# A GRU with a mixture of experts behind it: the router's two weight parts as one 16-column product, their sums added on GpSimd

## The chip, the cores and the metric

The kernel runs on one core of a Trainium2 chip. A core has TensorE (PE: matmuls, with weight loads, PEld, beside them), VectorE (DVE), ScalarE (ACT), GpSimd (POOL) and SyncE (SP, which here only starts transfers). Each engine works through its own instructions in order; they wait for one another by semaphores. The metric is the device time of one execution in microseconds.

## The reference

```python
# x: (16, 256, 512), the hidden state h: (16, 512), 256 time steps in sequence
gi = x_t @ W_ih + b_ih ;  gh = h @ W_hh + b_hh
r = sigmoid(i_r + h_r) ;  z = sigmoid(i_z + h_z) ;  n = tanh(i_n + r * h_n)
h = (1 - z) * n + z * h
# every h is then a token of a mixture of 8 experts, 2 of them used:
logits = h / max(|h|, 1e-12) @ router_w                # router_w: (512, 8)
w, e = top_k(softmax(logits), 2) ;  w = w / sum(w)
out = x + sum over e of combine[:, e] * (h @ Wa[e] @ Wb[e])   # ranks of 128
```

## The kernel before

**Precision.** Every fp32 operand of a matmul is split in a high and a low fp16 part. A product is made of three terms, high x high, high x low, low x high (`TERMS`), added up in PSUM.

**Stages.** The 256 time steps are taken eight at a time: a block is 8 steps x 16 batch rows = 128 tokens, and there are 32 blocks (`NB`). Step n is step s = n % 8 of block i = n // 8. In each step TensorE does the recurrence first (`state_part`, L958 and L963 for the reset and candidate gates, L969 and L973 for the update gate) and then, in `beside(n)`, filler from other blocks: one expert's first product for the block before (`expert_down`, L1014), a half of an input product (`n_part`, L912), one expert's second product (`expert_up`, L1037), and input products for later steps (`pair_part`, L883). In the step s = 3 it also computes the router's sums for the block before (`route`, L988 and L994).

**The recurrence.** VectorE waits for the gates (`rh_done`), transposes them (L762), adds the halves (L765, L768, L771), and, with ScalarE's sigmoids and tanh (L616, L620, L622, L624) between, makes the new state (L774 to L789; L788 writes the fp16 high part that TensorE multiplies next, L746 the low part). TensorE's L958 of the next step waits for L788 (`hhi_ready`).

**The router.** The 16-bit high and low parts of the block's states are in `hf`, those of the router's weights in `rw`, stored as `[128, part, k, 8]`. `route(f)` makes the sum of squares of each token (L988, three matmuls of one column) and the 8 logits (L994, 4 values of k x 3 terms = 12 matmuls of 8 columns), side by side in the bank `nbank`. ScalarE copies the 9 columns to `router` (L647, `router_read`), in its own `beside` of step s = 3, ahead of `split_y` (L658, L662), which reads an expert's product out of PSUM. GpSimd then makes the inverse norm (`invert_norm`, L465, L469), and VectorE ranks the logits (`rank_experts`, L796 and L798: the largest values and their indices). GpSimd takes the gap of the two largest (`gaps`, L474, L475) and copies the indices (L477). One step later ScalarE turns the gap into the two weights (`weigh`, L653) and GpSimd places them in `comb` (`combine`, L482 to L491), by which VectorE adds each expert's product to the result (`add_expert`, L815; the first one of a block waits for `comb`).

**The order around it.** The order of each engine is written out by hand, in each engine's `beside(n)` and, for the last block, `last_experts()`. On VectorE `rank_experts` stands in step s = 3 behind `gru_step` and `add_expert` and in front of the next step's `gru_step`; up to step 17 a piece of weight splitting (L741) follows it. On GpSimd in step s = 3 the order is: `less_upper_half`, `low_y` (L458, the low part of an expert's product, which waits for both of ScalarE's `split_y` reads), `invert_norm`, `gaps`.

Of the kernel before, what the change touches and what calls it, by code (L numbers as in the profile page):

```python
# [9 lines left out]
ALU = mybir.AluOpType  # L10
ACT = mybir.ActivationFunctionType

P = 128
PART_SCALE = 128.0
PROD_SCALE = PART_SCALE * PART_SCALE


TERMS = ((0, 0), (0, 1), (1, 0))
# [5 lines left out]
def wait(eng, sem, value):  # L24
    if value > 0:
        eng.wait_ge(sem, value)


def gru_moe_kernel(nc, x, cond, W_ih, W_hh, b_ih, b_hh, router_w, Wa, Wb, out):
    B, T, D = x.shape  # L30
    NE, _, R = Wa.shape
    K = D // P
    S = P // B
    NB = T // S
# [15 lines left out]
    with ExitStack() as ctx:  # L50
        def sb(name, shape, dt=F32):
            return ctx.enter_context(nc.sbuf_tensor(name, shape, dt))

        def ps(name, shape):
            return ctx.enter_context(nc.psum_tensor(name, shape, F32))

        def sem(name):
            return ctx.enter_context(nc.semaphore(name))
# [15 lines left out]
        rw = sb("rw", [P, 2, K, NE], F16)  # L74
# [45 lines left out]
        hf = sb("hf", [P, 2, K, P], F16)  # L120
# [3 lines left out]

        sqs = sb("sqs", [P, 3, P])
        ones_bf = sb("ones_bf", [P, 1], BF16)
        router = sb("router", [P, NE + 1])
        normf = sb("normf", [P, 1])
        rnorm = sb("rnorm", [P, 1])
        top = sb("top", [P, 8])  # L130
# [17 lines left out]
        nbank = ps("nbank", [P, 4 * P])  # L148
# [69 lines left out]
        sq_step = sem("sq_step")  # L218
        logits_done = sem("logits_done")
        router_read = sem("router_read")  # L220
        top_step = sem("top_step")
        gap_ready = sem("gap_ready")
        rnorm_step = sem("rnorm_step")
# [14 lines left out]
        def upper_half(part):  # L238
            return sqs[:, part, :].bitcast(BF16).rearrange("p (c h) -> p c h", h=2)[:, :, 1]
        SQ_STEPS, TOP_STEPS, RN_STEPS, COMB_STEPS = 4, 2, 2, 4  # L240
# [52 lines left out]
        def splits_before(n):  # L293
            return sum(len(SPLITS[i][4]) for i in range(n))
# [105 lines left out]
        def _(pool):  # L400
# [27 lines left out]
            def split_x(b, half, n):  # L428
                of = slice(half * D // 2, (half + 1) * D // 2)
                pool.wait_ge(xhi_ready, b + 1)  # L430
                pool.wait_ge(x_scaled, b - 2)
                pool.wait_ge(both_parts_ready, 2 * (n + 2))
                low = nc.gpsimd.tensor_tensor(xh[:, b % 2, 1, of], x128[:, of], xh[:, b % 2, 0, of], ALU.subtract)  # L433
                low.then_inc(xlo_ready if half else xlo_begun, 1)

            def fold_squares(f, n):
                pool.wait_ge(sq_ready, f + 1)
                if n < T:
                    pool.wait_ge(both_parts_ready, 2 * (n + 2))
                nc.gpsimd.tensor_tensor(sq2[:, :], sq[:, 0:2 * P], sq[:, 2 * P:4 * P], ALU.add).then_inc(sq_step, 1)  # L440

            def add_squares(f, n):
                pool.wait_ge(sq_step, f * SQ_STEPS + 1)
                wait(pool, logits_done, f)
                if n < T:
                    pool.wait_ge(both_parts_ready, 2 * (n + 2))
                nc.gpsimd.tensor_tensor(sqs[:, 0, :], sq2[:, 0:P], sq2[:, P:2 * P], ALU.add).then_inc(sq_step, 1)

            def less_upper_half(f, part):
                pool.wait_ge(sq_step, f * SQ_STEPS + 2 + part)  # L450
                nc.gpsimd.tensor_tensor(sqs[:, part + 1, :], sqs[:, part, :], upper_half(part), ALU.subtract
                                        ).then_inc(sq_step, 1)

            def low_y(m):
                pool.wait_ge(yhi_ready, m + 1)
                pool.wait_ge(y32_ready, m + 1)
                wait(pool, o_done, m - YB + 1)
                nc.gpsimd.tensor_tensor(y[:, m % YB, 1, :], y32[:, :], y[:, m % YB, 0, :], ALU.subtract  # L458
                                        ).then_inc(ylo_ready, 1)

            def invert_norm(f):

                r0, most = f * RN_STEPS, NORM_FLOOR * PROD_SCALE
                pool.wait_ge(router_read, f + 1)
                nc.gpsimd.tensor_scalar(normf[:, :], router[:, NE:NE + 1], PROD_SCALE, most * most, ALU.mult, ALU.max  # L465
                                        ).then_inc(rnorm_step, 1)
                pool.wait_ge(rnorm_step, r0 + 1)
                wait(pool, wt_ready, f)
                nc.gpsimd.tensor_tensor(rnorm[:, :], normf[:, :], root_pow[:, :], ALU.pow).then_inc(rnorm_step, 1)  # L469

            def gaps(f):
                pool.wait_ge(top_step, f * TOP_STEPS + 1)
                wait(pool, wt_ready, f)
                nc.gpsimd.tensor_tensor(gap[:, 0:1], top[:, 0:1], top[:, 1:2], ALU.subtract).then_inc(gap_ready, 1)  # L474
                nc.gpsimd.tensor_tensor(gap[:, 1:2], top[:, 1:2], top[:, 0:1], ALU.subtract).then_inc(gap_ready, 1)  # L475
                pool.wait_ge(top_step, (f + 1) * TOP_STEPS)
                nc.gpsimd.tensor_copy(top_no[:, :], top_at[:, :]).then_inc(gap_ready, 1)  # L477
# [28 lines left out]
            def beside(n):  # L506
                i, s = n // S, n % S
                if s == 1 and 1 <= i:
                    fold_squares(i - 1, n)
                if s == 2 and 1 <= i:  # L510
                    add_squares(i - 1, n)
                    less_upper_half(i - 1, 0)
                if s == 3 and 1 <= i:
                    less_upper_half(i - 1, 1)
                if s in (0, 4) and 1 <= i and i + 2 < NB:
                    split_x(i + 2, s // 4, n)
                if 0 <= n - DOWN:
                    low_y(n - DOWN)
                if s == 3 and 1 <= i:
                    invert_norm(i - 1)  # L520
                    gaps(i - 1)
                if s == 4 and 1 <= i:
                    combine(i - 1)

            def last_experts():
                fold_squares(NB - 1, T)
                add_squares(NB - 1, T)
                for part in range(2):
                    less_upper_half(NB - 1, part)
                for m in range(LAST, T):  # L530
                    low_y(m)
                    if m == LAST + 1:
                        invert_norm(NB - 1)
                        gaps(NB - 1)
                    if m == LAST + 2:
                        combine(NB - 1)

            for n in range(T):
                beside(n)
# [3 lines left out]
        def _(act):  # L543
# [98 lines left out]
            def read_router(f):  # L642
                act.wait_ge(logits_done, f + 1)

                wait(act, top_step, f * TOP_STEPS)
                wait(act, rnorm_step, f * RN_STEPS)
                nc.scalar.activation(router[:, :], nbank[:, P:P + NE + 1], ACT.Copy).then_inc(router_read, 1)  # L647

            def weigh(f):
                act.wait_ge(rnorm_step, (f + 1) * RN_STEPS)  # L650
# [80 lines left out]
        def _(dve):  # L731
# [58 lines left out]
                high_low(n)  # L790

            def rank_experts(f):
                dve.wait_ge(router_read, f + 1)

                wait(dve, gap_ready, 3 * f)
                nc.vector.max(top[:, :], router[:, 0:NE]).then_inc(top_step, 1)  # L796
                dve.wait_ge(top_step, f * TOP_STEPS + 1)
                nc.vector.max_index(top_at[:, :], top[:, :], router[:, 0:NE]).then_inc(top_step, 1)  # L798
# [52 lines left out]
        def _(pe):  # L851
# [126 lines left out]
            def route(f):  # L978

                if f == 0:  # L980
                    pe.wait_ge(weights_split, splits_before(N_RW_SPLITS))
                if f == NB - 2:
                    pe.wait_ge(gi_ready, K * NB)

                wait(pe, router_read, f)
                pe.wait_ge(sq_step, (f + 1) * SQ_STEPS)
                for part in range(3):
                    nc.tensor.matmul(nbank[:, P + NE:P + NE + 1], upper_half(part), ones_bf[:, :],  # L988
                                     start=(part == 0), stop=(part == 2), skip_group_check=True)
                pe.wait_ge(hf_ready, 2 * (f + 1))  # L990
                n = 0
                for k in range(K):
                    for ph, pw in TERMS:
                        mm = nc.tensor.matmul(nbank[:, P:P + NE], hf[:, ph, k, :], rw[:, pw, k, :], start=(n == 0),  # L994
                                              stop=(n == 3 * K - 1), skip_group_check=True)
                        n += 1
                mm.then_inc(logits_done, 1)

            def expert_down(m):
# [73 lines left out]
            for g, n_cols in ((gates[0], 2), (gates[1], 2), (zbank, 1)):  # L1073
                for c in range(n_cols):
                    mm = nc.tensor.matmul(g[:, c * P:(c + 1) * P], zeros, zeros, start=(c == 0), stop=(c == n_cols - 1),
                                          skip_group_check=True)
# [37 lines left out]
```

## Time and profile before

| | us |
|---|---|
| median of 3 runs | 1042.89 (1042.72 to 1044.01) |
| span of the profiled execution | 1040.8 |
| TensorE matmul busy | 1011.4 (97%) |
| VectorE busy | 860.0 (83%) |
| ScalarE busy | 722.6 (69%) |
| GpSimd busy | 299.0 (29%) |

The profiled execution is a run by itself. The page gives its span, first to last instruction, and no separate device time for it. Matmuls are pipelined: the row of a matmul shows its whole way through the array, 166 ns for one of L994, while the next one starts long before it ends; so the cost of a matmul in a full stream is the distance from one start to the next, and the chain of waits counts by that distance. A bracket behind a row of the timeline gives the idle time of the engine before it and what ended it.

### The profile page before, as it was taken

The page shows a single profiled execution, that of the slowest core. Times are in us where ns is not written, and L with a number is a line of the kernel's source. Part 1 is how long each engine was busy: PE and PEld are TensorE (multiplying, and loading weights), DVE is VectorE, ACT ScalarE, POOL GpSimd, SP SyncE. Part 2 cuts the span into 40 slices and gives each one's busy share as a digit, 9 for nine tenths or more (in the row PEclk, how much of TensorE's full clock was granted, in tenths as well). Part 3 has the DMA queues.
Part 4 walks back from the last instruction along what each step waited for, and adds up shares of the span by engine and source line. Part 5 has one row for each costly group of instructions (what it writes and reads, how often), then busy time and mean ns, then how long its engine had stood idle before and what let it go on. Part 6 is the DMA issues. An engine that isn't in the chain of part 4 may idle for free.

```text
span 1040.8 us, 67010 instructions
## 1 busy us (share of the span) xinstructions
PE 1011.4 (97%) x28409; PEld 828.4 (80%) x28409; DVE 860.0 (83%) x3215; ACT 722.6 (69%) x2824; POOL 299.0 (29%) x762
## 2 busy tenths in 40 slices
PE   5789999999999999999999999999999999999997
PEld 3677888888888888888888888888888888888875
DVE  6889888888888888888888888888888888888886
ACT  7687666767666767667767667667766767766663
POOL 2032232322233332233332233332233332223223
PEclk9999999999999999999999999999999999999999
DMA  8230111111111111111111111111111011110001
GB/s 295 84 94 17 30 32 29 30 27 30 29 32 29 29 27 30 29 32 30 29 28 28 29 32 32 27 30 27 29 32 32 26 30 28 29 32 20 9 9 33
DMA packets 49522, 39.24 MB, mean 38 GB/s; under 512 B 34676, under 2 KB 39112, under 8 KB 49224
## 3 DMA queue, kind: packets, MB, share of 16 engines
q1 hardware_dynamic: 48376, 31.41, 11.1%
q8 instruction: 226, 3.70, 1.5%
q10 hardware_dynamic: 848, 3.54, 1.0%
q14 instruction: 72, 0.59, 0.2%
HBM read 18.94 MB, written 8.39 MB: 26 GB/s over the span
## 4 chain that ended last, share of the span: by engine, by line
PE 91%; DVE 5%; ACT 2%; DMA 1%; issue 1%; POOL 0%; ACTq 0%; DVEq 0%; POOLq 0%
PE ybank L1014 18%; PE pairs L883 17%; PE obank L1037 15%; PE gates L958 11%; PE gates L963 10%; PE nbank L912 7%; PE zbank L973 5%; PE zbank L969 5%; DVE tr L762 1%; PE nbank L994 1%; DMA wih<-in_L_cond_W_ih 1%; DVE pre L765 1%; DVE acc L815 1%; ACT nn L624 1%; DVE pre L771 1%
## 5 line engine op out<-in xcount | busy, mean ns | idle before, releaser
L883 PEld LDWEIGHTS pairs<-wx,xs 128*32 128x32 f16 x6144 | 140.7, 96 | 105.8 <-issue 101.7
L883 PE MATMUL pairs<-wx,xs 128*32 128x256 f16 x6144 | 215.6, 275 | 0.0
L1014 PE MATMUL ybank<-hparts,wa 128*128 128x128 f16 x3024 | 212.5, 220 | 0.0
L458 POOL TENSOR_TENSOR y<-y 128x128 f16<-128x128 f32 x256 | 111.7, 436 | 348.1 <-ACT y L658 190.0
L1037 PE MATMUL obank<-wb,y 128*128 128x512 f16 x738 | 199.3, 379 | 0.0
L1014 PEld LDWEIGHTS ybank<-hparts,wa 128*128 128x128 f16 x3024 | 169.8, 98 | 26.9
L762 DVE STREAM_TRANSPOSE tr<-gates 128x256 f32<-128x256 f32 x256 | 115.1, 450 | 72.4 <-PE gates L963 68.5
L616 ACT ACTIVATE rr<-pre 128x64 f32<-128x64 f32 x256 | 65.7, 257 | 155.6 <-DVE pre L765 155.2
L958 PE MATMUL gates<-whh,st 128*32 128x256 f16 x4080 | 155.8, 273 | 11.3 <-DVE st L788 10.8
L963 PE MATMUL gates<-whh,hparts 128*32 128x256 f16 x4080 | 155.9, 273 | 0.0
L815 DVE SCALAR_TENSOR_TENSOR acc<-obank,comb,acc 128x512 f32<-128x512 f32 x184 | 136.9, 744 | 0.2
L912 PE MATMUL nbank<-xs,win 128*128 128x128 f16 x1488 | 123.5, 219 | 0.0
L958 PEld LDWEIGHTS gates<-whh,st 128*32 128x32 f16 x4080 | 107.6, 97 | 19.9 <-issue 17.7
L611 ACT ACTIVATE hparts<-st 128x64 f16<-128x64 f16 x257 | 65.9, 257 | 81.8 <-DVE st L788 81.5
L578 ACT ACTIVATE gates<-pairs,step_rows 128x256 f32<-128x256 f32 x256 | 115.3, 450 | 0.3 <-PE pairs L883 0.3
L963 PEld LDWEIGHTS gates<-whh,hparts 128*32 128x32 f16 x4080 | 109.6, 97 | 2.0
L620 ACT ACTIVATE zz<-pre 128x64 f32<-128x64 f32 x256 | 65.6, 256 | 58.6 <-DVE pre L771 58.5
L973 PE MATMUL zbank<-whh,hparts 128*32 128x128 f16 x4080 | 101.4, 219 | 0.0
L969 PE MATMUL zbank<-whh,st 128*32 128x128 f16 x4080 | 101.4, 219 | 0.0
L784 DVE SCALAR_TENSOR_TENSOR u<-nn,omz 128x64 f32<-128x64 f32 x256 | 57.5, 225 | 43.9 <-ACT nn L624 43.8
L433 POOL TENSOR_TENSOR xh<-x,xh 128x256 f16<-128x256 f32 x58 | 39.8, 686 | 187.9 <-DVE hparts L746 187.9
L912 PEld LDWEIGHTS nbank<-xs,win 128*128 128x128 f16 x1488 | 93.2, 98 | 0.7
(134 smaller groups left out, 1701.4 us busy)
## 6 DMA issues: line engine op xcount, KB each, us to landing
out<-outb SPq DMA_DIRECT2D x63, 128.0 KB
xin<-in_x SPq DMA_DIRECT2D x58, 128.0 KB
wih<-in_L_cond_W_ih ACTq DMA_DIRECT2D x4, 768.0 KB, 7.7
whh<-in_L_cond_W_hh SPq DMA_DIRECT2D x4, 768.0 KB, 11.8
wih<-in_L_ffn_Wb SPq DMA_DIRECT2D x8, 256.0 KB, 2.7
xs<-xh SPq DMA_TRANSPOSE x116, 2.8
wih<-in_L_ffn_Wa SPq DMA_DIRECT2D x4, 256.0 KB, 4.2
whh<-in_L_ffn_Wa SPq DMA_DIRECT2D x4, 256.0 KB, 2.6
```

Of the source, the lines that this page charges most:

```text
L458: nc.gpsimd.tensor_tensor(y[:, m % YB, 1, :], y32[:, :], y[:, m % YB, 0, :], ALU.subtract).then_inc(ylo_ready, 1)
L578: nc.scalar.activation(gates[n % 2][:, 0:2 * P], pairs[n // 2 % 2][:, 0:2 * P], ACT.Copy, scale=step_rows[:, q:q + 1]).then_inc(seeded, 1)
L762: nc.vector.transpose(tr[:, 0:2 * K, :].rearrange("p (g k) c -> p g k c", k=K), g[:, 0:2 * P].rearrange("p (g c k) -> p g k c", g=2, k=K)) ...
L815: nc.vector.scalar_tensor_tensor(out=(outb if e == NE - 1 else acc)[:, :], in0=o_at(m)[:, :], scalar=comb[:, e:e + 1], in1=(xin[:, f % XIN ...
L883: mm = nc.tensor.matmul(bank[32 * j:32 * j + 32, P:3 * P], turned(b, k, ph)[:, t0:t0 + 2 * B], wx[:, pw, k, j, :], start=False, stop=(k == ...
L912: mm = nc.tensor.matmul(n_at(b, m)[:, 0:P], win[:, pw, k, m, :], turned(b, k, ph), start=(i == 0), stop=(i == 11), skip_group_check=True)
L958: nc.tensor.matmul(g[32 * j:32 * j + 32, 0:2 * P], st[:, k, :], whh[:, 1, k, j, 0:2 * P], start=False, stop=False, skip_group_check=True)
L963: mm = nc.tensor.matmul(g[32 * j:32 * j + 32, 0:2 * P], prior[:, k, :], whh[:, 0, k, j, 0:2 * P], start=False, stop=(k == K - 1), skip_gro ...
L969: nc.tensor.matmul(zbank[32 * j:32 * j + 32, 0:P], st[:, k, :], whh[:, 1, k, j, 2 * P:3 * P], start=False, stop=False, skip_group_check=True)
L973: mm = nc.tensor.matmul(zbank[32 * j:32 * j + 32, 0:P], prior[:, k, :], whh[:, 0, k, j, 2 * P:3 * P], start=False, stop=(k == K - 1), skip ...
L1014: mm = nc.tensor.matmul(y_at(m)[:, 0:P], wa[:, pw, k, e, :], hparts[:, f % HB, k, :, ph * B:(ph + 1) * B], start=(n == 0), stop=(n == 3 * ...
L1037: mm = nc.tensor.matmul(o_at(m)[:, :], y[:, m % YB, ph, :], wb[:, pw, m % NE, :], start=(n == 0), stop=(n == 2))
```

## The change

The three router terms are grouped by the state's part. With the high part of the states as the stationary operand, one matmul per k multiplies both parts of the router's weights at once, 16 columns: columns 0 to 7 get high x high, columns 8 to 15 high x low. With the low part, one matmul per k adds low x high to columns 0 to 7. That makes 4 + 4 = 8 matmuls in place of 12, and leaves two groups of 8 sums, plus the squares in column 16. ScalarE copies all 17 columns into a new tile `sums`. A new function on GpSimd, `sum_logits`, adds the two groups into `router`, now 8 columns wide, and raises a new semaphore, `logits_summed`. VectorE's `rank_experts` waits for that one in place of `router_read`; `read_router` waits for the addition of the block before, and `sum_logits` for the ranking of the block before.

```diff
-        router = sb("router", [P, NE + 1])
+        sums = sb("sums", [P, 2 * NE + 1])
+        router = sb("router", [P, NE])
...
+            def sum_logits(f):
+                pool.wait_ge(router_read, f + 1)
+                wait(pool, top_step, f * TOP_STEPS)
+                nc.gpsimd.tensor_tensor(router[:, :], sums[:, 0:NE], sums[:, NE:2 * NE], ALU.add
+                                        ).then_inc(logits_summed, 1)
...
-                nc.gpsimd.tensor_scalar(normf[:, :], router[:, NE:NE + 1], PROD_SCALE, most * most, ALU.mult, ALU.max
+                nc.gpsimd.tensor_scalar(normf[:, :], sums[:, 2 * NE:2 * NE + 1], PROD_SCALE, most * most, ALU.mult, ALU.max
...
                 if s == 3 and 1 <= i:
+                    sum_logits(i - 1)
                     invert_norm(i - 1)
                     gaps(i - 1)
...
                     if m == LAST + 1:
+                        sum_logits(NB - 1)
                         invert_norm(NB - 1)
...
-                wait(act, top_step, f * TOP_STEPS)
+                wait(act, logits_summed, f)
                 wait(act, rnorm_step, f * RN_STEPS)
-                nc.scalar.activation(router[:, :], nbank[:, P:P + NE + 1], ACT.Copy).then_inc(router_read, 1)
+                nc.scalar.activation(sums[:, :], nbank[:, P:P + 2 * NE + 1], ACT.Copy).then_inc(router_read, 1)
...
             def rank_experts(f):
-                dve.wait_ge(router_read, f + 1)
+                dve.wait_ge(logits_summed, f + 1)
...
-                    nc.tensor.matmul(nbank[:, P + NE:P + NE + 1], upper_half(part), ones_bf[:, :],
+                    nc.tensor.matmul(nbank[:, P + 2 * NE:P + 2 * NE + 1], upper_half(part), ones_bf[:, :],
...
-                n = 0
-                for k in range(K):
-                    for ph, pw in TERMS:
-                        mm = nc.tensor.matmul(nbank[:, P:P + NE], hf[:, ph, k, :], rw[:, pw, k, :], start=(n == 0),
-                                              stop=(n == 3 * K - 1), skip_group_check=True)
-                        n += 1
+                for part in range(2):
+                    for k in range(K):
+                        mm = nc.tensor.matmul(nbank[:, P:P + (2 - part) * NE], hf[:, part, k, :], rw[:, 0:2 - part, k, :],
+                                              start=(part == 0 and k == 0), stop=(part == 1 and k == K - 1),
+                                              skip_group_check=True)
                 mm.then_inc(logits_done, 1)
```

## Rows read from the trace of the kernel before

**Rows 1.** The page: busy time of each engine; the chain's shares by engine.
```profile
PE 1011.4 (97%) x28409; PEld 828.4 (80%) x28409; DVE 860.0 (83%) x3215; ACT 722.6 (69%) x2824; POOL 299.0 (29%) x762
PE 91%; DVE 5%; ACT 2%; DMA 1%; issue 1%; POOL 0%; ACTq 0%; DVEq 0%; POOLq 0%
```

**Rows 2.** Table by stretch: busy us of each engine, granted clock, DMA.
```profile
core 0: us, PE busy (x) PEld busy (x) DVE busy (x) ACT busy (x) POOL busy (x), PEclk, DMA share, GB/s
105.00:990.00 885.00, 885.00 (x25211) 731.02 (x25200) 737.15 (x2811) 617.66 (x2466) 261.02 (x654) 1.00 0.11 29
990.00:1021.00 31.00, 29.24 (x805) 22.38 (x803) 26.38 (x104) 19.48 (x82) 7.99 (x21) 1.00 0.05 15
```

**Rows 3.** Chain of waits, 507 to 513 us: start, us, what.
```profile
507.42 0.05 PE nbank L988 x3
507.47 0.30 PE nbank L994 x12
...
509.21 0.44 PE gates L958 x16
...
511.31 0.34 PE nbank L912 x6
...
513.06 0.21 PE gates L958 x5
```

**Rows 4.** Timeline around one ranking: start, us, instruction, operands.
```profile
508.80 0.16 ACT L647 ACTIVATE router<-nbank 128x9 f32<-128x9 f32 x1
...
508.91 0.75 DVE L815 SCALAR_TENSOR_TENSOR acc<-obank,comb,acc 128x512 f32<-128x512 f32 x1
...
509.43 0.43 POOL L458 TENSOR_TENSOR y<-y 128x128 f16<-128x128 f32 x1 [2.66 <-ACT y L658]
...
509.57 0.16 DVE L796 MAX8 top<-router 128x8 f32<-128x8 f32 x1
...
509.94 0.26 POOL L465 TENSOR_SCALAR normf<-router 128x1 f32<-128x1 f32 x1
...
510.14 0.45 DVE L762 STREAM_TRANSPOSE tr<-gates 128x256 f32<-128x256 f32 x1
```

**Rows 5.** Timeline of GpSimd, one step earlier.
```profile
505.98 0.43 POOL L458 TENSOR_TENSOR y<-y 128x128 f16<-128x128 f32 x1
506.37 0.40 POOL L451 TENSOR_TENSOR sqs<-sqs 128x128 f32<-128x128 f32 x1
```

**Rows 6.** Groups by line, 105 to 990 us: busy us, mean ns, idle before.
```profile
L578 ACT ACTIVATE gates<-pairs,step_rows 128x256 f32<-128x256 f32 x227 | 102.4, 451 | 0.0
...
L662 ACT ACTIVATE y<-ybank 128x128 f32<-128x128 f32 x227 | 61.4, 270 | 0.0
...
L491 POOL TENSOR_TENSOR comb<-pick 128x8 f32<-128x8 f32 x29 | 6.0, 207 | 2.4
```

**Rows 7.** Timeline of the closing experts: a GpSimd result and its user.
```profile
1029.64 0.20 POOL L491 TENSOR_TENSOR comb<-pick 128x8 f32<-128x8 f32 x1
...
1029.94 0.75 DVE L815 SCALAR_TENSOR_TENSOR acc<-pairs,comb,xin 128x512 f32<-128x512 f32 x1 [1.91 <-PE pairs L1037]
```

**Rows 8.** Timeline of the step behind the thirty-first ranking.
```profile
1007.38 0.43 POOL L458 TENSOR_TENSOR y<-y 128x128 f16<-128x128 f32 x1 [2.25 <-ACT y L658]
...
1008.15 0.45 DVE L762 STREAM_TRANSPOSE tr<-gates 128x256 f32<-128x256 f32 x1 [0.19 <-PE gates L963]
...
1011.86 0.45 DVE L762 STREAM_TRANSPOSE tr<-gates 128x256 f32<-128x256 f32 x1 [0.20 <-PE gates L963]
```

**Rows 9.** Timeline around the first ranking.
```profile
71.70 0.17 DVE L796 MAX8 top<-router 128x8 f32<-128x8 f32 x1
...
72.06 0.67 DVE L741 SCALAR_TENSOR_TENSOR wb<-wih,wb 128x512 f16<-128x512 f32 x1
72.15 0.88 POOL L458 TENSOR_TENSOR y<-y 128x128 f16<-128x128 f32 x1 [2.12 <-ACT y L662]
...
75.27 0.62 PE L958 MATMUL gates<-whh,st 128*32 128x256 f16 x16 [0.42 <-DVE st L788]
```

**Rows 10.** Chain of waits in the closing experts.
```profile
1025.60 0.30 PE nbank L994 x12
...
1033.18 0.66 PE gates L1037 x3
```

More of the change, by code:

```diff
@@ L220, in gru_moe_kernel @@
         router_read = sem("router_read")
+        logits_summed = sem("logits_summed")
         top_step = sem("top_step")
```

## Prediction, made before the change was run

> **What bounds the kernel now.** I read the page first, for the engine whose work fills the span. TensorE (PE) is busy 97% of it and makes up 91% of the chain that ended last [rows 1]. The share alone proves little, so the second view is the stretch table: between 105 and 990 us TensorE is busy for all 885.00 us, at a granted clock of 1.00, the 2.4 GHz level [rows 2]. In it lie the steps behind 29 of the 32 routings (comb's addition, which comes in that step, is counted x29) [rows 6]; there every matmul taken away is time saved, unless something else then comes last. The third view is the chain around one block's routing. The twelve routing matmuls (L994) take 0.30 us in it, 25 ns each, with no gap before or after, and from one step's first state matmul (L958) to the next is 3.85 us (509.21 to 513.06) [rows 3]. A block is eight such steps and the 0.35 us of L988 and L994, 31.15 us.
>
> The question is how much VectorE (DVE) may be late before that unbroken chain breaks. Each step is a loop: VectorE turns the gates (L762), computes the new state, TensorE multiplies it. The end of the kernel shows the loop bare, because TensorE has less filler there: L762 to L762 is 1008.15 to 1011.86, 3.71 us, in just the step that follows a ranking [rows 8]. So against TensorE's 3.85 us per step VectorE has 0.14 us to spare, once, before TensorE waits for the new state (L788 to L958). This is the number that the change has to live within.
>
> **The change, part by part.**
>
> *Matmuls.* Twelve become eight per block: four of 16 columns (high state times both weight parts), four of 8. The spacing is 25 ns at 8 columns [rows 3]. For 16 columns the trace has no row; below stands 25 ns, above the line from 25 ns at 8 columns to 57 ns at 128 (six L912 in 0.34 us), which gives 27 ns. I take 25, nearest by far. Saved: 4 x 0.025 = 0.10 us per block, all on TensorE's path in the 29 blocks.
>
> *ScalarE's read* (L647) goes from 9 to 17 columns. An evacuation costs 270 ns for 128 columns and 451 ns for 256 [rows 6], 1.4 ns a column, so 8 more are 0.01 us (bounds 0 and 0.02). ScalarE's next two reads (L658, L662) feed GpSimd's low_y, so this 0.01 us delays all below.
>
> *The new GpSimd addition, and the wait for it.* Now VectorE ranks as soon as its add_expert is over: MAX8 at 509.57, right behind L815, which ran 508.91 to 509.66. The sums had long been there (L647 at 508.80) [rows 4]. After the change MAX8 waits for logits_summed. GpSimd works in order, and the diff puts sum_logits behind low_y (L458), which starts at 509.43. Queued behind MAX8 on VectorE is the next step's L762, the head of the recurrence; TensorE waits for that. Step by step from low_y's start:
> - low_y to the addition: 0.39 us, as between two GpSimd additions (505.98 to 506.37) [rows 5]. The next instruction there now, the norm's TENSOR_SCALAR, comes 0.51 us behind (509.43 to 509.94) [rows 4]; that is the upper bound. It is another form, so I take 0.39.
> - the addition: 0.20 us, as comb's addition of the same shape, 207 ns [rows 6]. Above, 0.43 us, low_y's 128 columns; the 8-column row is nearest.
> - GpSimd to VectorE: L491 ends at 1029.84 and the first L815 of a block, which waits for comb, starts at 1029.94, 0.10; I take 0.09 for the rounding [rows 7]. Bounds 0 and 0.10.
> - MAX8 until the next VectorE instruction can start: 71.70 to 72.06, 0.36 us for both ranking instructions [rows 9].
>
> Sum 0.39 + 0.20 + 0.09 + 0.36 = 1.04, with the wider read 1.05 us. L762 now starts 0.71 us after low_y (510.14 less 509.43) [rows 4], and it isn't held by the ranking but by TensorE's gates. So L762 comes 0.34 us late. The loop absorbs 0.14; TensorE stands 0.20 us late against now. The 0.10 us of matmuls is not to be taken off again: it was gained before this wait, and a wait that ends at a time set by VectorE's earlier work swallows it (L762's arrival is counted from the old clock). After that the step is TensorE's again. Per block +0.20, and 29 x 0.20 = +5.8 us.
>
> *The first routing (f = 0)* lies where VectorE sets the pace: TensorE waits 0.42 us for the new state in the step after it [rows 9]. There nothing is absorbed. MAX8 is at 71.70 now and would be at 72.15 + 0.39 + 0.20 + 0.09 + 0.01 = 72.84: +1.14 us, with the weight split L741 queued behind it. I count the addition from 0.39 behind low_y's start although low_y takes 0.88 us there: L741 ran beside it from 72.06, and after the change L741 comes later than both. If low_y still took 0.88, add 0.45.
> A rule bears on this row. The Trainium skill's SBUF — State Buffer (SBUF: two separate sides) says that GpSimd and a VectorE instruction with two SBUF inputs hold one port pair exclusively. The trace agrees: low_y takes 0.88 us beside L741 and 0.43 elsewhere. By the rule the steady blocks pay nothing extra, since VectorE stands idle from 509.66 while the addition runs.
>
> *The thirty-first routing (f = 30)* is in the stretch where VectorE paces again: low_y 1007.38, L762 1008.15, 0.77 apart [rows 8]; 1.05 less 0.77 is +0.28 us, nothing absorbed.
>
> *The last routing* runs beside the closing experts, where TensorE works on until 1033.84 [rows 10]. GpSimd's chain (norm, weights, comb, low_y) gets 0.2 us longer, TensorE's 0.10 shorter. VectorE's five last additions leave room. I take 0, bounds -0.1 and +0.2.
>
> Everything else that moves has cover: GpSimd's norm and gaps come 0.2 to 0.35 us later, and their user, the weights' sigmoid, one step (3.8 us) later; the extra wait of read_router is for the block before; no DMA is added, and none is issued behind MAX8 (SP's transfers follow h_ready, so they move with the step).
>
> The Trainium skill's GPSIMD Engine Reference (4.1 Engine selection) sends elementwise additions to VectorE and puts GpSimd at about 2x for two inputs, which speaks against this change. By that, an addition at twice VectorE's 157 ns MAX8 would be an estimated 0.31 us, and the sum 31 x 0.11 = 3.4 us higher; the 207 ns row of the same shape decides against it, and the place in the queue costs more than the duration.
>
> **Sum.** 1.14 + 5.8 + 0.28 + 0 = +7.2 us on the profiled span of 1040.8, so 1048.0. The median of the three runs, 1042.89, lies 2.1 us above that span, which I take for what lies around it: 1042.89 + 7.2 = 1050.1 us.
>
> **Rivals.**
> *A, the ranking is covered.* If the addition came early enough, only the matmuls would count: 31 x 0.10 = -3.1 us, 1039.8, faster. The deciding point: MAX8 no later than 0.71 + 0.14 - 0.10 - 0.36 = 0.39 us after low_y's start. For it: TensorE is full, and the saving is on its path. Against: 0.39 us is where the addition would only begin. It needs GpSimd to take no time, or to be ahead of low_y, and it is in order.
> *B, GpSimd starts the addition as late as it now starts the norm.* 0.51 for 0.39 is +0.12 in all 31 loops: 7.2 + 3.7 = 10.9, 1053.8 us. For it: the row at that very place. Against: that row and the other one behind low_y with this gap are TENSOR_SCALAR; addition behind addition is 0.39.
> *C, a smaller loss.* The handoff near 0 and the read free: -0.10 x 31, 1047.0 us; if VectorE's spare were also 0.2 us instead of 0.14, 1045.3. The loop's 3.71 us speaks against the latter.
> *D, the clock.* If TensorE's new pauses cost it its clock, many us. Against: from 990 to 1021 us it pauses in every step and is granted 1.00 [rows 2].
>
> **From this the numbers.** Forecast (1048 to 1052) 0.57, B 0.18, C 0.15, A and what lies between A and no change 0.06, dearer than B (a 0.43 us addition, D) 0.04. The range that holds 8 in 10 reaches from C to B: 1046.0 to 1054.0. About 0.2% (2.1 us) is what a measurement can tell from no change; faster by more 0.04, within 0.05, slower 0.91.
>
> **What would show it.** In a middle block: eight L994-type matmuls in 0.20 us; GpSimd's addition 0.39 us behind low_y, 0.2 long; MAX8 some 0.68 us behind low_y's start, VectorE idle before it with GpSimd named; L762 some 0.33 us behind MAX8; TensorE waiting at L958 of the step after that, on VectorE's L788, once per block; block to block 31.35 instead of 31.15 us. The prediction fails if TensorE has no such wait, if MAX8 lies before low_y's end, or if the loss comes in a step other than the one behind the ranking.

## The result, and the profile after

The changed kernel takes 1048.03 us (median of 4 runs, 1047.58 to 1048.49) against 1043.08 for the kernel before on the same chip: a ratio of 1.0047, 95% interval 1.0033 to 1.0062. It is slower by about 5 us; 7.2 were forecast. The profiled execution is one of the longer two of its four (1048.42 us, span 1046.6).

The page has little to say about it: TensorE is at 97% as before [rows 1], GpSimd is busy 5 us more.

```profile
PE 1012.4 (97%) x28281; PEld 824.0 (79%) x28281; DVE 861.6 (82%) x3215; ACT 722.8 (69%) x2824; POOL 303.8 (29%) x794
PE 90%; DVE 6%; ACT 2%; issue 1%; DMA 1%; POOL 0%; ACTq 0%; DVEq 0%; POOLq 0%
```

The table by stretch shows the first trace of it. Where TensorE was busy for every microsecond [rows 2], it now has pauses, 1.63 us in 888, and its clock is untouched:

```profile
core 0: us, PE busy (x) PEld busy (x) DVE busy (x) ACT busy (x) POOL busy (x), PEclk, DMA share, GB/s
107.00:995.00 888.00, 886.37 (x25079) 726.02 (x25067) 737.88 (x2811) 617.87 (x2465) 264.98 (x683) 1.00 0.11 29
```

The pauses are in one place, in front of L968, the first state product (L958 before), in the step behind a ranking: 27 of them, about 0.06 us each. They are less than half of the loss; the rest hides in matmuls that take longer, as shown below. This is the timeline around the ranking that answers to [rows 4] (start, us, instruction, idle before it and what ended that):

```profile
512.38 0.74 DVE L825 SCALAR_TENSOR_TENSOR acc<-obank,comb,acc 128x512 f32<-128x512 f32 x1
...
512.90 0.43 POOL L460 TENSOR_TENSOR y<-y 128x128 f16<-128x128 f32 x1 [2.67 <-ACT y L668]
...
513.28 0.20 POOL L466 TENSOR_TENSOR router<-sums 128x8 f32<-128x8 f32 x1
...
513.52 0.17 DVE L806 MAX8 top<-router 128x8 f32<-128x8 f32 x1 [0.40 <-POOL router L466]
...
513.88 0.43 DVE L772 STREAM_TRANSPOSE tr<-gates 128x256 f32<-128x256 f32 x1
...
517.58 0.45 DVE L772 STREAM_TRANSPOSE tr<-gates 128x256 f32<-128x256 f32 x1 [0.20 <-PE gates L973]
```

The addition (L466) starts 0.38 us behind low_y (L460). VectorE stands idle for 0.40 us, until 0.03 us behind the addition's end, then ranks, and the transpose of the next step's gates (L772, L762 before) comes 0.98 us behind low_y's start, where it had been 0.71. The list of waits has this one 32 times, once per block:

```profile
DVE top L806 <- POOL router L466: 13.5, 32, 1.1
```

In the chain of waits TensorE pays for it one step later: a gap in front of L968 and a longer L968, where [rows 3] has 0.44.

```profile
512.56 0.44 PE gates L968 x16
...
515.64 0.77 PE pairs L893 x24
516.41 0.07 issue
516.48 0.62 PE gates L968 x16
517.10 0.44 PE gates L973 x16
```

The gap of 0.07 us and the 0.18 us by which L968 is longer are 0.25 us together. The views do not name VectorE as what ended this gap, so here are the two instructions themselves, the write of the new state (L788, now L798) and TensorE's first use of it, before and after:

```profile
512.37 0.22 DVE L788 TENSOR_TENSOR st<-u,v 128x64 f16<-128x64 f32 x1
...
512.88 0.61 PE L958 MATMUL gates<-whh,st 128*32 128x256 f16 x16
```
```profile
516.10 0.23 DVE L798 TENSOR_TENSOR st<-u,v 128x64 f16<-128x64 f32 x1
...
516.48 0.62 PE L968 MATMUL gates<-whh,st 128*32 128x256 f16 x16
```

Before, the state lay ready for 0.29 us when TensorE took it up; now it is taken up 0.15 us after its write ends. 0.15 us is also what the trace shows in the steps from 37 to 45 us in the kernel before, where TensorE stands idle for 1.0 us and the views name L788 as what ended it. So in this step TensorE waits for VectorE, and the 0.14 us between the two figures is what the loop had to spare.

### The profile page after: what moved, and what is told of

Same layout as the page of the kernel before. It is cut to its first block, busy times and chain, and to the rows that moved or that the text cites. A ratio compares the mean times of both kernels' runs of the same rounds, so it can differ in the third digit from the quotient of the medians.

```text
span 1046.6 us, 66817 instructions
## 1 busy us (share of the span) xinstructions
PE 1012.4 (97%) x28281; PEld 824.0 (79%) x28281; DVE 861.6 (82%) x3215; ACT 722.8 (69%) x2824; POOL 303.8 (29%) x794
## 4 chain that ended last, share of the span: by engine, by line
PE 90%; DVE 6%; ACT 2%; issue 1%; DMA 1%; POOL 0%; ACTq 0%; DVEq 0%; POOLq 0%
PE ybank L1023 17%; PE pairs L893 17%; PE obank L1046 14%; PE gates L968 11%; PE gates L973 10%; PE nbank L922 7%; PE zbank L983 5%; PE zbank L979 5%; DVE tr L772 1%; DMA wih<-in_L_cond_W_ih 1%; DVE pre L775 1%; PE nbank L1003 1%; DVE acc L825 1%; ACT nn L634 1%; DVE tr L778 1%
## 5 line engine op out<-in xcount | busy, mean ns | idle before, releaser
L460 POOL TENSOR_TENSOR y<-y 128x128 f16<-128x128 f32 x256 | 111.1, 434 | 346.0 <-ACT y L668 191.0
L968 PE MATMUL gates<-whh,st 128*32 128x256 f16 x4080 | 156.5, 273 | 14.6 <-DVE st L798 12.2
L772 DVE STREAM_TRANSPOSE tr<-gates 128x256 f32<-128x256 f32 x256 | 114.5, 447 | 63.1 <-PE gates L973 62.7
L968 PEld LDWEIGHTS gates<-whh,st 128*32 128x32 f16 x4080 | 106.0, 96 | 30.1 <-issue 28.0
```

The costliest lines, as they stand in the source:

```text
L772: nc.vector.transpose(tr[:, 0:2 * K, :].rearrange("p (g k) c -> p g k c", k=K), g[:, 0:2 * P].rearrange("p (g c k) -> p g k c", g=2, k=K)) ...
L968: nc.tensor.matmul(g[32 * j:32 * j + 32, 0:2 * P], st[:, k, :], whh[:, 1, k, j, 0:2 * P], start=False, stop=False, skip_group_check=True)
```

## The experiments

Each kernel starts from the changed one. Where a table or a sentence gives the length of a step, it runs from one transpose of the gates (L762 in the kernel before) to the next, worked out from their starts in the trace, as the median of 26 middle blocks. The cuts of the edits leave lines out at "...".

**e4, the matmuls alone.** The addition is taken out, and the ranking reads the first group:

```diff
-                dve.wait_ge(logits_summed, f + 1)
+                dve.wait_ge(router_read, f + 1)
...
-                nc.vector.max(top[:, :], router[:, 0:NE]).then_inc(top_step, 1)
+                nc.vector.max(top[:, :], sums[:, 0:NE]).then_inc(top_step, 1)
...
```

> The eight matmuls and the 17-column read alone: no addition anywhere, VectorE ranks the first group of 8 sums, so the high x low term is left out of the logits. Theory: 31.06 us per block, 0.10 us less than before, MAX8 right behind add_expert; median about 1040.0. Rival 1 (the 16-column matmuls are dearer than 25 ns, or the read): not faster than before, 1043 or more.

Measured: 1039.94 us, 0.9971 of the kernel before (0.9961 to 0.9982), 31.06 us per block. Chain of waits of e4, eight matmuls in 0.20 us, 25 ns each, four of them 16 columns wide:

```profile
506.40 0.05 PE nbank L990 x3
506.45 0.20 PE nbank L995 x8
506.65 0.67 PE obank L1038 x3
```

The wide product is worth what was forecast for it, 0.10 us per block. The loss lies wholly in how the two groups come together.

**e3, the wait without the saving.** Twelve matmuls again. In this kernel the second group's start leaves the high x high term of k = 0 out of the first group.

```diff
-                for part in range(2):
-                    for k in range(K):
-                        mm = nc.tensor.matmul(nbank[:, P:P + (2 - part) * NE], hf[:, part, k, :], rw[:, 0:2 - part, k, :],
+                for k in range(K):
+                    for ph, pw in TERMS:
+                        mm = nc.tensor.matmul(nbank[:, P + pw * NE:P + (pw + 1) * NE], hf[:, ph, k, :], rw[:, pw, k, :],
...
+                                              start=(k == 0 and ph == 0), stop=(k == K - 1), skip_group_check=True)
```

> The changed kernel with twelve matmuls of 8 columns again (high x low goes to the second group of columns), all else as changed: the wait without the saving. Theory: the wait ends at a time that VectorE and GpSimd set, so the four matmuls are free here: 31.30 us per block as in the changed kernel, median 1048.0 to 1048.3. Rival 4 (saving and wait add up): 31.40 us per block, 1051.1.

Measured: 1047.84 us (1.0047, 1.0033 to 1.006), 31.29 us per block; the changed kernel has 31.30. The chain of waits of e3 has the 0.10 us back in the matmuls and less in the step after:

```profile
511.36 0.30 PE nbank L1003 x12
...
516.18 0.77 PE pairs L893 x24
516.95 0.58 PE gates L968 x16
```

Under this wait four matmuls per block are free. Saving and wait do not add up: the time at which the new state is ready is set by VectorE and GpSimd, and TensorE merely waits longer or shorter for it: its pause and its L968 take 0.69 us in the changed kernel and 0.58 in e3.

**e5, more lateness.** Two more additions on GpSimd in front of the one that counts:

```diff
...
+                for t in range(2):
+                    nc.gpsimd.tensor_tensor(spare[:, t, :], expert_no[:, :], expert_no[:, :], ALU.add)
                 nc.gpsimd.tensor_tensor(router[:, :], sums[:, 0:NE], sums[:, NE:2 * NE], ALU.add
```

> The changed kernel with two more additions of 128x8 on GpSimd, right before the one of the sums, into a tile that nobody reads. Theory (all of GpSimd's time behind low_y is paid in full past the 0.15 us that the loop spares): each pushes the ranking back by about 0.155 us (206 ns less the 50 ns by which such additions overlap), so 31.61 us per block against 31.30 of the changed kernel, +9.6 us over 31 routings, 1057.6. Rival (the loss in the changed kernel is a fixed price of a handoff, or of a wide product, and not of lateness): 1048 to 1050.

Measured: 1057.40 us, 31.60 us per block. Timeline of e5:

```profile
516.46 0.43 POOL L461 TENSOR_TENSOR y<-y 128x128 f16<-128x128 f32 x1 [2.66 <-ACT y L671]
516.84 0.36 POOL L468 TENSOR_TENSOR spare<-expert_no 128x8 f32<-128x8 f32 x2
517.16 0.20 POOL L469 TENSOR_TENSOR router<-sums 128x8 f32<-128x8 f32 x1
517.39 0.17 DVE L809 MAX8 top<-router 128x8 f32<-128x8 f32 x1 [0.70 <-POOL router L469]
```

0.32 us more in front of the sum, 0.30 us more per block. A fixed price (1048 to 1050) is out; the loss follows the lateness.

**e2, the addition in front of low_y.**

```diff
+                if s == 3 and 1 <= i:
+                    sum_logits(i - 1)
                 if 0 <= n - DOWN:
                     low_y(n - DOWN)
                 if s == 3 and 1 <= i:
-                    sum_logits(i - 1)
                     invert_norm(i - 1)
```

> The changed kernel with GpSimd's addition moved in front of low_y in step 3 (the last block stays as it is). Theory: the addition then ends near 0.2 us before low_y would start, the ranking begins right behind add_expert as in the kernel before, no wait at all: 31.06 us per block, median about 1040.0. Rival 1 (wide matmuls): 1047 to 1049. Rival 3 (GpSimd's share itself: more work on it, the port it shares with VectorE, the handoff): the loss stays wholly or in part, 1044 to 1048.

Measured: 1040.46 us, 0.9976 (0.9967 to 0.9985), 31.06 us per block: the saving of e4 with the sum kept. Timeline of e2:

```profile
507.92 0.75 DVE L826 SCALAR_TENSOR_TENSOR acc<-obank,comb,acc 128x512 f32<-128x512 f32 x1
...
508.04 0.20 POOL L466 TENSOR_TENSOR router<-sums 128x8 f32<-128x8 f32 x1 [2.27 <-ACT sums L658]
...
508.43 0.43 POOL L460 TENSOR_TENSOR y<-y 128x128 f16<-128x128 f32 x1 [0.18 <-issue]
...
508.58 0.16 DVE L807 MAX8 top<-router 128x8 f32<-128x8 f32 x1
```

MAX8 has no wait in front of it. It is the same instruction on the same engine, and only its place in GpSimd's queue differs. About 0.4 us of its distance to e4 is the first block: there the ranking follows no add_expert, so it does wait, and that step takes 4.44 us against e4's 4.05 (in e6 4.65, which is as much as e6 lies above e4). Timeline of e2 there:

```profile
71.91 0.17 DVE L807 MAX8 top<-router 128x8 f32<-128x8 f32 x1 [0.28 <-POOL router L466]
```

**e10, the ranking one step later.** The addition stays behind low_y; VectorE's ranking and GpSimd's gaps move to step s = 4.

```diff
                     sum_logits(i - 1)
                     invert_norm(i - 1)
+                if s == 4 and 1 <= i:
                     gaps(i - 1)
-                if s == 4 and 1 <= i:
                     combine(i - 1)
...
-                if s == 3 and 1 <= i <= NB:
+                if s == 4 and 1 <= i <= NB:
                     rank_experts(i - 1)
```

> The changed kernel, GpSimd's addition where it was (behind low_y), but VectorE ranks one step later (s = 4, behind that step's add_expert), and GpSimd's gaps move with it. Theory (the cost lies in what is queued behind the wait, not in the addition or its place): the sums have long been there, the ranking's 0.36 us fits in the 0.33 us that VectorE idles before each transpose and the loop's 0.15 us, no wait: 31.06 us per block, and no loss behind the first ranking; median about 1039.9. Rival (GpSimd's addition behind low_y costs something by itself): 1043 or more. What could spoil it: the weights come 3.8 us later on ScalarE and GpSimd, and comb must be there for the next step's add_expert; if it is not, up to 0.5 us per block is lost.

Measured: 1041.51 us, 0.9984 (0.9974 to 0.9993), 31.06 us per block. Timeline of e10, one step behind the addition:

```profile
513.06 0.15 DVE L806 MAX8 top<-router 128x8 f32<-128x8 f32 x1
```

So the late addition by itself costs nothing; what costs is the recurrence queued behind the wait. The spoiler did not come in the middle blocks. "No loss behind the first ranking" was a miss: there the three steps from s = 3 on take 3.95 + 4.17 + 4.73 us against 4.05 + 3.72 + 4.20 in e4, 0.88 us more. In them the weight split that follows the ranking (L751) takes 1.12 us beside a GpSimd addition, where it had 0.67 in the kernel before [rows 9]. The median lies 1.6 us above that of e4 (the eleven times go from 1040.7 to 1042.1), and the rest of that stays open.

**e1 and e6, the addition on VectorE.** e1 moves it there as it is, in front of the ranking:

```diff
+                dve.wait_ge(router_read, f + 1)
+                wait(dve, top_step, f * TOP_STEPS)
+                nc.vector.tensor_tensor(router[:, :], sums[:, 0:NE], sums[:, NE:2 * NE], ALU.add
+                                        ).then_inc(logits_summed, 1)
                 dve.wait_ge(logits_summed, f + 1)
```

> The changed kernel with the addition of the two groups of 8 sums on VectorE, directly in front of its ranking, and none on GpSimd. Theory (the wait): what costs is that VectorE's next transpose of the gates comes 0.29 us late behind a ranking that waits for GpSimd. With the addition on VectorE it starts right behind add_expert, the ranking 0.19 us later, and the next transpose may be 0.09 us late, less than the 0.15 us that the loop has to spare: TensorE never waits, block to block 31.06 us (31.16 before, 31.30 changed), median about 1040.4. Rival 1 (wide matmuls): the cost is in the 16-column product or the 17-column read; then the loss stays, 1047 to 1049. Rival 2 (any more work ahead of the transpose costs its full length): +0.2 us per block less 0.1, 1046.

Measured: 1042.83 us, 1.0003 (0.9994 to 1.0012), 31.15 us per block. That is a miss: I had given VectorE's addition about 0.16 us, and it took twice that. Timeline of e1, and the line's durations (min/median/max, ns):

```profile
509.50 0.43 POOL L460 TENSOR_TENSOR y<-y 128x128 f16<-128x128 f32 x1 [2.66 <-ACT y L660]
509.64 0.30 DVE L797 TENSOR_TENSOR router<-sums 128x8 f32<-128x8 f32 x1
509.98 0.17 DVE L802 MAX8 top<-router 128x8 f32<-128x8 f32 x1
```
```profile
L797 DVE TENSOR_TENSOR router<-sums x32: 154/303/402, 71.6 to 1026.1; 128x8 f32<-128x8 f32 x32
```

It ends 0.02 us behind low_y. It does so in 30 of the 32 blocks, also in the one where it started 0.05 us behind low_y's start instead of 0.15 and took 402 ns; in the two others it started ahead of low_y and took 166 and 154 ns. Hence e6, with a reduction of one 16-wide input in its place:

```diff
-                nc.vector.tensor_tensor(router[:, :], sums[:, 0:NE], sums[:, NE:2 * NE], ALU.add
-                                        ).then_inc(logits_summed, 1)
+                nc.vector.tensor_reduce(router[:, :], sums[:, 0:2 * NE].rearrange("p (h e) -> p e h", h=2),
+                                        mybir.AxisListType.X, ALU.add).then_inc(logits_summed, 1)
```

> As e1_vector_adds, but VectorE adds the two groups by a reduction over one input of 128x16 in place of an addition of two inputs. In e1 the addition ran into GpSimd's low_y and took a median of 303 ns where its shortest took 154. Theory 1 (two inputs in SBUF are what made it wait for low_y): the reduction takes 150 to 180 ns beside low_y, the ranking starts about 0.2 us behind add_expert, the next transpose is under 0.02 us late, 31.06 us per block, 1040.2. Theory 2 (any VectorE read of this kind waits for low_y, or PSUM and the semaphore are to blame): 300 ns again and 31.15 us per block, 1042.8.

Measured: 1040.56 us, 0.9975 (0.9964 to 0.9985), 31.06 us per block. Timeline of e6, and its durations:

```profile
509.11 0.43 POOL L460 TENSOR_TENSOR y<-y 128x128 f16<-128x128 f32 x1 [2.66 <-ACT y L660]
509.25 0.16 DVE L797 TENSOR_REDUCE router<-sums 128x8 f32<-128x16 f32 x1
509.44 0.17 DVE L802 MAX8 top<-router 128x8 f32<-128x8 f32 x1
```
```profile
L797 DVE TENSOR_REDUCE router<-sums x32: 155/159/171, 72.1 to 1024.3; 128x8 f32<-128x16 f32 x32
```

Beside the same low_y, with one input, it takes 159 ns. Theory 1 holds. The transpose is still 0.10 us later than in e4, and the loop absorbs that: the step is 4.225 us and the next one 3.747.

**All of them on one line.** The table has two steps in us: s3 to s4, in which the ranking lies, and s4 to s5. "Late" is by how much the first is longer than in e4, so how late the transpose of s4 comes; "lost" is what both together are longer.

| kernel | s3 to s4 | s4 to s5 | late | lost |
|---|---|---|---|---|
| e4, e2, e10 | 4.125 | 3.847 | 0 | 0 |
| e6 | 4.225 | 3.747 | 0.100 | 0.000 |
| e1 | 4.364 | 3.696 | 0.239 | 0.088 |
| changed | 4.517 | 3.694 | 0.392 | 0.239 |
| e5 | 4.815 | 3.695 | 0.690 | 0.538 |

Lost is late less 0.15, and nothing below that. (The kernel before has 4.225 and 3.847: its 0.10 us over e4 are four matmuls on TensorE's own path, not lateness, and nothing absorbs them.) The changed kernel's 0.239 less the 0.10 us that the matmuls save is the +0.14 us per block (31.16 to 31.30).

## Why the prediction was right

- *What bounds the kernel, and 25 ns per matmul at 16 columns*: right (e4).
- *The mechanism*: right. The ranking waits for GpSimd, which is held by low_y; the next transpose is late; TensorE waits one step later, once per block. e2 and e10 take the lateness away in two independent ways and both keep the saving.
- *The saving is swallowed, not subtracted*: right (e3 and the changed kernel, 31.29 and 31.30).
- *Addition 0.39 us behind low_y, 0.20 us long*: 0.387 and 0.206 in the middle blocks. The norm's 0.51 (rival B) was the other form's. The wider read, put at 0.01, costs 0.006 us (ScalarE's 162 ns became 168).
- *Handoff from GpSimd to VectorE, 0.09 us*: wrong size. From the addition's end to MAX8 it is 0.03 us in the middle blocks. I had read it off [rows 7], and the row itself says otherwise: the bracket behind L815 names the matmuls of L1037 as what ended its wait, not comb. The error is 0.06 us in each of 31 loops, 1.9 us, most of what I forecast too much. The small handoff was rival C's condition, and the measured 1048.03 lies nearer to its 1047.0 than to my 1050.1; it is only just inside the 1048 to 1052 that I held likeliest.
- *The sign at L958*: right in substance, not in form. I had announced a wait for L788 named once per block; the views name it in no middle block, and it shows by the state being taken up 0.15 us after its write. No clock was lost (rival D): 1.00 in the middle stretch.
- *The loop's spare, 0.14*: 0.15. Started late, the loop takes 3.694 us, not the 3.71 of [rows 8].
- *First ranking +1.14, thirty-first +0.28*: +1.08 and +0.20 (the two steps behind it, 4.286 + 3.693 against 4.065 + 3.711). As forecast, low_y went back there from 0.88 to 0.43 us.
- *29 middle blocks*: 28. In the block of the second routing low_y starts earlier in the step (0.94 us ahead of the transpose, not 0.71), and that pair of steps gets 0.09 us shorter. I counted it like the others without looking.
- *The closing experts 0*: from the last transpose to the end, 0.13 us less.

Together 1.08 - 0.09 + 28 x 0.143 + 0.20 - 0.13 = +5.06 us, against 4.95 measured between the medians. The profiled spans differ by 5.8; 0.8 us of that lies in front of the first routing, where the two programs do the same (see below).

Three kernels with the whole sum beat the kernel before: e2, e6 and e10, with 0.9976, 0.9975 and 0.9984 of its time. Their floor is e4 with 0.9971.

## What to carry to other kernels

A wait placed at the head of an in-order queue is paid by what stands behind it; ask what that is, and how much the loop through it can spare, before asking how long the awaited thing takes. When a result is handed to another engine, its place in that engine's queue counts more than its duration: here the kernel with the same 0.2 us addition loses 5 us when it stands behind low_y and gains 2.5 when it stands in front. Take a handoff's price only from a row whose bracket names that handoff.

## What the runs showed of the hardware that I had not expected

A VectorE addition of two 8-column inputs in SBUF took 303 ns beside GpSimd's addition and 154 at its shortest, where it started ahead of it; a reduction of one 16-column input took 159 beside it. It works the other way too. In the changed kernel GpSimd's power (L477) takes 1.09 us beside VectorE's weight split (L751), where it has 0.57 us in the middle blocks:

```profile
73.98 0.67 DVE L751 SCALAR_TENSOR_TENSOR wb<-wih,wb 128x512 f16<-128x512 f32 x1
74.00 1.09 POOL L477 TENSOR_TENSOR rnorm<-normf,root_pow 128x1 f32<-128x1 f32 x1
```

This is the exclusive pair of ports of the Trainium skill (SBUF — State Buffer, SBUF: two separate sides). I had cited that rule and not applied it to my own first experiment.

The first steps vary by about 1 us from one profile to the next. TensorE's granted clock is half, the 1.2 GHz level, for a stretch early on, and where that stretch falls differs. In the kernel before it begins near 25.5 us, ahead of the first step's transpose (27.5 us), after a stretch of 1.5 us in which TensorE was busy for 0.45; in the changed kernel's profile it begins near 30 us, after 1.2 us in which TensorE was busy for 0.05, and lies in the first two steps, which take 4.62 + 3.88 us in place of 3.78 + 3.71. The tables of the kernel before and of the changed one:

```profile
25.50:28.80 3.30, 3.11 (x65) 2.05 (x66) 2.72 (x8) 1.79 (x7) 0.00 (x0) 0.50 0.19 58
30.00:33.30 3.30, 3.05 (x100) 2.58 (x100) 2.74 (x11) 2.56 (x10) 0.00 (x0) 1.00 0.38 102
```
```profile
25.50:28.80 3.30, 2.44 (x68) 1.74 (x68) 2.73 (x9) 1.90 (x8) 0.00 (x0) 1.00 0.34 102
30.00:33.30 3.30, 3.30 (x71) 2.87 (x72) 2.06 (x7) 1.62 (x6) 0.00 (x0) 0.50 0.35 102
```

e3 has the slow first steps as well, and the other six do not, so it does not go with the change. What moves the stretch was not tested.
